# Three hand-written orders per engine in place of two, with the experts' bias product behind the small tiles, in a software-pipelined four-layer kernel

## The reference

```python
x = x + xattn0(layernorm(x), ctx, ctx)   # 16 heads of 8, biases
x = x + moe(layernorm(x))                # 8 experts, top 2, relu
x = x + xattn1(layernorm(x), ctx, ctx)   # 16 heads of 8, no biases
x = x + cell(layernorm(x))               # 64 steps over the rows of a group
# moe: scores = xf @ W_gate + b_gate; w = top-2 scores at their experts, else 0
#      h = relu(xf @ W1[e] + b1[e]); out = sum_e w[e] * (h @ W2[e] + b2[e])
# cell, one step, batch of 64:
#      f = sigmoid(xt @ wf.T + c @ uf.T + bf); i = sigmoid(xt @ wi.T + c @ ui.T + bi)
#      g = tanh(xt @ wc.T + c @ uc.T + bc);    c = f * c + i * g
# after the last step: h = tanh(x @ wo.T + c_final @ uo.T + bo)
```

## Time and profile before

| what | value |
|---|---|
| median of three runs | 847.08 us |
| the three runs | 846.52, 847.08, 849.42 us |
| span of the profiled execution, first to last instruction | 848.5 us |
| TensorE products, busy | 822.1 us (97%) |
| ScalarE busy | 783.1 us (92%) |
| VectorE busy | 769.7 us (91%) |
| GpSimd busy | 686.1 us (81%) |

### The profile page before, as it was taken

How to read it: one execution, slowest core, us unless ns; L and a number is a source line. 1 busy time by engine, 2 the same in 40 slices (tenths; PEclk the granted TensorE clock), 3 DMA queues, 4 the chain that set the end, 5 groups by cost and what they waited for, 6 DMA issues and landing times. The chain is left out here.

```text
span 848.5 us, 41475 instructions
## 1 busy us (share of the span) xinstructions
PE 822.1 (97%) x15268; PEld 739.4 (87%) x15268; DVE 769.7 (91%) x2778; ACT 783.1 (92%) x2490; POOL 686.1 (81%) x1292
## 2 busy tenths in 40 slices
PE   7899999999999999999999999999999999999996
PEld 4688898999999999999999899999998988888784
DVE  5689999999999999999999999999999998999755
ACT  4899999999999999999999999999999999988864
POOL 4788998888888888888888888888888887877634
PEclk7899999999999999999999999999999999999999
DMA  9400000000000000000000000000000000000005
GB/s 348 166 2 3 2 3 4 3 3 4 3 4 3 3 3 3 4 3 4 3 3 3 3 4 3 3 4 3 3 3 3 4 3 3 3 4 3 3 3 199
DMA packets 6965, 17.67 MB, mean 21 GB/s; under 512 B 752, under 2 KB 2288, under 8 KB 6768
## 3 DMA queue, kind: packets, MB, share of 16 engines
q1 hardware_dynamic: 6336, 14.36, 4.4%
q10 hardware_dynamic: 432, 0.68, 0.2%
HBM read 10.84 MB, written 4.19 MB: 18 GB/s over the span
## 5 line engine op out<-in xcount | busy, mean ns | idle before, releaser
L976 DVE TENSOR_REDUCE mx<-ps 128x8 f32<-128x512 f32 (+1 forms) x288 | 166.8, 621 | 11.9 <-PE ps L366 11.8
L1305 POOL TENSOR_TENSOR h<-Ex 128x512 f32<-128x512 f32 (+1 forms) x144 | 166.0, 1153 | 10.7 <-ACT Ex L734 8.1
L990 DVE TENSOR_TENSOR Ex<-ps,mx 128x512 f32<-128x512 f32 (+1 forms) x288 | 167.4, 622 | 0.0
L745 ACT ACTIVATE ET<-ps 128x512 f32<-128x512 f32 (+1 forms) x288 | 155.3, 573 | 11.1 <-PE ps L381 8.9
L734 ACT ACTIVATE Ex<-Ex 128x512 f32<-128x512 f32 (+1 forms) x288 | 163.8, 596 | 0.0
L1082 DVE SCALAR_TENSOR_TENSOR acc<-ps,we,acc 128x128 f32<-128x128 f32 x448 | 150.9, 337 | 11.9 <-PE ps L467 0.5
L783 ACT ACTIVATE hT<-ps,w 128x128 f32<-128x128 f32 x512 | 149.0, 400 | 4.7 <-PE ps L446 4.6
L381 PE MATMUL ps<-w,Ex 128*128 128x128 f32 x1024 | 149.8, 275 | 1.5 <-ACT qT L722 0.7
L446 PEld LDWEIGHTS ps<-xT,w 128*128 128x128 f32 x1024 | 124.1, 191 | 24.8 <-issue 24.6
L446 PE MATMUL ps<-xT,w 128*128 128x128 f32 x1024 | 142.2, 282 | 0.0
L467 PE MATMUL ps<-w,hT 128*128 128x128 f32 x1024 | 139.5, 281 | 0.3 <-DVE Ex L990 0.3
(11 more groups left out here) (108 smaller groups left out, 1793.7 us busy)
## 6 DMA issues: line engine op xcount, KB each, us to landing
cx<-ctx_dram SPq DMA_DIRECT2D x7, 512.0 KB, 12.3
x<-x_dram SPq DMA_DIRECT2D x7, 512.0 KB, 14.1
out_dram<-x SPq DMA_DIRECT2D x14, 256.0 KB, 2.7
w<-weights_dram SPq DMA_DIRECT2D x2, 512.0 KB, 5.8
w<-weights_dram SPq DMA_DIRECT2D x1, 576.0 KB, 8.5
out_dram<-x SPq DMA_DIRECT2D x4, 128.0 KB, 2.6
w<-weights_dram ACTq DMA_DIRECT2D x1, 328.0 KB, 5.2
w<-weights_dram ACTq DMA_DIRECT2D x1, 256.0 KB, 3.1
```

Source lines behind the costliest of these rows:

```text
L745: e.activation(ET[:, j % 2, r, lo:hi, :, :], b[:, 256 * lo:256 * hi].rearrange("p (c w q) -> p c w q", c=hi - lo, w=2), ACT.Copy).then_inc ...
L976: e.tensor_reduce(mx[:, j % 2, r, 4 * lo:4 * hi], b[:, 256 * lo:256 * hi].rearrange("p (j k) -> p j k", k=64), AX.X, ALU.max).then_inc(sig ...
L990: e.tensor_tensor(Ex[:, j % 2, r, 256 * lo:256 * hi].rearrange("p (j k) -> p j k", k=64), b[:, 256 * lo:256 * hi].rearrange("p (j k) -> p ...
L1305: e.tensor_tensor(u, v[:, :, :, 0:32], v[:, :, :, 32:64], ALU.add).then_inc(sig("half1"), 1)
```

## The change

Each engine gets three lists in place of two, for rounds 0 to 14, 15 to 71 and 72 to 79 (`STARTS`), with new orders in all of them, new lags where an operation moved from the end of a list to its head, and a new `AHEAD` with an entry for each of the three parts. `USES` has three tables. In TensorE's list of the full rounds `sA` comes before `pv`, `yb` comes right behind them and before `y0`, `q` and `rt` come between `gate` and `turnw`, and `e1` stands where `e0` stood. The pieces of b2 (`bias_pieces`) and the sum into `bo0` still stand at the head of VectorE's round, but the list behind them begins with `mx0` in place of `sb1`. No operation is added or taken out; no shape changes. `out_inputs` counts its groups from `OUT` = 73, the same round as before.

```diff
-FULL, LATE = FIRST, NT + -1
+STARTS = (0, 15, 72)
+FIRST, LAST = STARTS[0], 80
+OUT = NT + 9
 ...
 def phase(i):
-    return 0 if i < FULL else 1 if i < LATE else 2
+    return max(sum(i >= s for s in STARTS) - 1, 0)
 ...
+AHEAD = {"y0": (0, 0, -1), "wx0": (-1, -2, 1), "turnx": (0, 0, -1), "e1": (0, 0, -1), "p": (0, 0, -1),
 ...
```

More of the change, by code:

```diff
@@ L221, in build @@
         for i in range(FIRST, LAST):
-            for name, reader, lag, chain, step, first in (USES_LAST if i >= LATE else USES):
+            for name, reader, lag, chain, step, first in USES[phase(i)]:
                 made = 0
@@ L232, in build @@
                         made += 1
-                place += max(made, 1)
+                place += max(made, i >= 0)
         def bank_of(name, j):
@@ L499, in inputs_share @@
                 if m == 0:
-                    for name, reader, _, chain, step, first in USES:
+                    for name, reader, _, chain, step, first in USES[0]:
                         if name != "turnx":
@@ L589, in tensor_program @@
                     keys_values(r)
-            for i in range(LATE, LAST):
+            for i in range(STARTS[2], LAST):
+                for r in due(i, "turnw"):
+                    turn_w(r)
+                for r in due(i, "gate"):
+                    gate(r)
+                for r in due(i, "h0"):
+                    hidden(r, 0)
+                for r in due(i, "e1"):
+                    turn_e(r, 1)
+                for r in due(i, "p"):
+                    project(r)
+                for r in due(i, "turnx"):
+                    turn_x(r)
+                for r in due(i, "y1"):
+                    experts(r, 1)
@@ new lines, in tensor_program @@
+                for r in due(i, "h1"):
+                    hidden(r, 1)
+                for r in due(i, "e3"):
+                    turn_e(r, 3)
+                for r in due(i, "xin"):
+                    cell_inputs(r)
+                for r in due(i, "S"):
+                    scores(r)
+                for r in due(i, "sA"):
+                    step(r, 0)
+                for r in due(i, "pv"):
+                    values(r)
+                for r in due(i, "rt"):
+                    turn_r(r)
@@ L598, in tensor_program @@
+                for r in due(i, "wx0"):
+                    out_inputs(r, 0)
                 for r in due(i, "sB"):
                     step(r, 1)
[L600 to L610, removed]
@@ L626, in tensor_program @@
[L626 to L630, removed]
+                for r in due(i, "yb"):
+                    expert_bias(r)
             for n in (5, 6):
@@ L834, in scalar_program @@
                     e.wait_ge(sig("cell"), 1)
[L835 to L840, removed]
-                    exps(r, 0)
+                for r in due(i, "xo1"):
+                    out_inputs(r, 1)
+                for r in due(i, "re1"):
+                    relus(r, 1)
+                for r in due(i, "gB"):
+                    gates(r, 1)
+                for r in due(i, "sc"):
+                    scale(r)
                 for r in due(i, "ex1"):
                     exps(r, 1)
+                for r in due(i, "kvc"):
+                    keys_values(r)
+                for r in due(i, "ET3"):
+                    turn_e(r, 3)
                 for r in due(i, "qc"):
@@ L857, in scalar_program @@
                     turn_w(r)
+                for r in due(i, "ex2"):
+                    exps(r, 2)
+                for r in due(i, "xo0"):
+                    out_inputs(r, 0)
+                for r in due(i, "gA"):
+                    gates(r, 0)
+                for r in due(i, "rT"):
+                    turn_r(r)
+                for r in due(i, "ex3"):
+                    exps(r, 3)
+                for r in due(i, "re0"):
+                    relus(r, 0)
+            for i in range(STARTS[1], STARTS[2]):
+                for r in due(i, "re1"):
+                    relus(r, 1)
+                for r in due(i, "sc"):
+                    scale(r)
+                for r in due(i, "kvc"):
+                    keys_values(r)
+                for r in due(i, "ex0"):
+                    exps(r, 0)
+                for r in due(i, "gA"):
+                    gates(r, 0)
+                for r in due(i, "ET3"):
+                    turn_e(r, 3)
+                for r in due(i, "xT"):
+                    turn_x(r)
+                for r in due(i, "ET1"):
+                    turn_e(r, 1)
+                for r in due(i, "wd"):
+                    widen(r)
+                for r in due(i, "xo1"):
+                    out_inputs(r, 1)
+                for r in due(i, "ET0"):
+                    turn_e(r, 0)
+                for r in due(i, "ex1"):
+                    exps(r, 1)
+                for r in due(i, "ex2"):
+                    exps(r, 2)
+                for r in due(i, "ET2"):
+                    turn_e(r, 2)
+                for r in due(i, "qc"):
+                    query(r)
+                for r in due(i, "rT"):
+                    turn_r(r)
+                for r in due(i, "weT"):
+                    turn_w(r)
+                for r in due(i, "xo0"):
+                    out_inputs(r, 0)
+                for r in due(i, "gB"):
+                    gates(r, 1)
+                for r in due(i, "ex3"):
+                    exps(r, 3)
+                for r in due(i, "re0"):
+                    relus(r, 0)
@@ L1170, in vector_program @@
-                for r in due(i, "gidx"):
-                    gate_index(r)
+                for r in due(i, "sb0"):
+                    differences(r, 0)
+                for r in due(i, "c5"):
+                    combine(r, 5)
+                for r in due(i, "c7"):
+                    combine(r, 7)
+                for r in due(i, "mx1"):
+                    maxima(r, 1)
+                for r in due(i, "mx2"):
+                    maxima(r, 2)
+                for r in due(i, "st0"):
+                    stats_inputs(r)
```

443 lines of the change are left out of this document (264 added, 179 removed), and 73 rows, old and new, of tables (AHEAD, LAG, USES, USES_LAST).

## The result

| | median us | lowest to highest | runs |
|---|---|---|---|
| before, beside it | 847.20 | 846.52 to 849.42 | 5 |
| changed | 842.06 | 840.55 to 844.32 | 5 |

The ratio is 0.9933, interval 0.9914 to 0.9952: the change takes 5.1 us off where 4.3 were forecast. The profiled execution of the changed kernel has a span of 838.8 us and a time of 840.55, the shortest of the five. Before's profiled span of 848.5 thus belongs to a time of some 850.3, longer than all five of the table. The two profiles differ by 9.7 us, 4.6 of them because each lies at its own end of the scatter.

A forecast was written before the change was run, and what follows sets the result against it. TensorE's instructions in their order were taken to bound full rounds, a chain through all engines the start. Terms +4.8 - 3.9 - 0.8 - 3.5 - 0.9 = -4.3 us, from 847.08 to 843; range 836 to 852.

The forecast's parts named there:

- rival 3: Full rounds: q is late, so scores waits each round; at 0.3 us a round 857; chance 0.17.
- rival 1: Full rounds: array partly hides q's and h0's loads, round 11.98 to 12.0, 838; chance 0.24, shared with a better start.
- (a): Full round, yb moved ahead of y0: uncovered loads 0.16 after and 0.16 before, worth nothing, -0.01 to +0.06.
- (d): Full round: sA ahead of pv, e1 ahead of p and e0, the two wx calls: neighbours of one kind, 0.
- (b): Full round, gate: q's f32 load now follows its 8-column product and is uncovered, +0.075 (0.03 to 0.10).
- (c): Full round, turnw: h0's full products follow in place of two transposes, 0.33 against 0.29, +0.04.
- Rival 4: Full rounds: yb's bf16 load costs the 0.10 of an f32 one, 0.06 more a round, 846; chance 0.07.
- -0.8 for rounds 64 to 71: Eight rounds now in the full order: one run of small tiles fewer, -0.2, less 0.10 each; 0 to -1.6.
- the earlier wx0: Last rounds: wx0 issued one round earlier, its first eight products fill TensorE's idle time near 789; -0.9 (+2 to -2).
- rival 2: Start gives nothing, as several chains at once hold its rounds: 846.5, no measurable change; chance 0.16.
- (f): Start, rounds 4 to about 8: ex0 after xT (-0.3) and gate after e2 alone (0.15), 0.45 x 5 rounds = -2.2.
- (e): Start, VectorE: pieces of b2 and bo0 sum leave the softmax run for idle time before scores lands, -1.3.

The follow-up runs named there:

- second pair of profiles: Both kernels profiled again, unchanged: the changed kernel 841.52 us (ratio 0.9929), the kernel before 847.62 us (0.9999).
- the run with the wrong banks: Changed kernel with yb put back behind e3 in both program and bank table (USES[1]): 1044.56 us, ratio 1.2321.

## Why the prediction came out right, step by step

**The full round: right, 12.08 forecast and 12.085 measured.** (The +4.8 takes 0.10 a round for the 0.105 of the sum; 48 of these are 5.0.) All engines follow; no wait stands in the steady rounds (rival 3 is out, and so is rival 1). Of its terms: (a) yb, 0, measured -0.04, and (d) sA ahead of pv, 0, measured +0.03, by the run with yb back and the old banks: two errors of some 2 us each over 57 rounds that cancel, which is luck. yb's load behind the small tiles, put at 0.05, adds 0.01 to yb's slot; the 0.05 by which y0's load sticks out was right. (b) q behind the gate, +0.075, measured +0.08 in its slot. (c) turnw ahead of h0, +0.04, measured +0.05 - 0.01. The versions with q alone and with q and turnw moved give it back in part and in full, 2.6 to 3.1 and 4.3 to 4.8 us. Rival 4 falls with (a). A rule of the Trainium skill ("TensorE: Matmul & The Clock Gate", section "LDWEIGHTS (loading the stationary operand)") gives a load's time by its columns alone; by it yb's load, taken to delay its product in full, would cost as much as y0's, and the four slots together would have grown by about 0.06. They shrank by 0.01, and by 0.04 against the run with yb back, so this trace doesn't bear out the rule for what a load costs here. How long the load itself lasts is another matter: its record behind gate is 0.12 us long, and its product starts 0.02 after it.

What step (a) got wrong is its reading of the edit. I priced yb's move as a matter of weight loads and of neighbours in TensorE's queue. The two runs with yb back show that more hangs on it elsewhere: c0's new place on VectorE needs yb early (0.8 us a round if it isn't, 49 us in all), and the bank table turns with it (with both, 2.6 us a round, 4.3 where the clock falls). "Every instruction is kept; only its neighbours change" held for the time of this change, not for this part of it alone.

**Rounds 62 and 63: right, -3.9 forecast, -3.9 in the second pair of profiles.** The changeover at 66 shows the cause by itself.

**The rest of the last third: too good.** -0.8 for rounds 64 to 71 was +0.1 between tiles 63 and 70 (0.0 in the first pair). The full-list rounds with fewer stages cost more at first (tiles 63 to 66, 34.5 in the changed kernel, where the last list takes 33.9) and as much less later. I had priced entries and exits of small tiles, not the two lists; what a saved run of small tiles gives there, no run shows. -0.9 for the earlier wx0 was -0.6 between tiles 70 and 76, but not by wx0: its first group comes 6.6 us behind tile 70, where the idle time of the earlier trace rows lay 1.9 us behind it. The whole last list is new, and which of its moves gives the 0.6 is open; at its start it costs 1.6 us, and gives back more in the next rounds. TensorE's waits in the 104 us up to tile 76 fell from 3.2 us to 2.6.

**The start: -3.5 forecast, -4.1 measured, by the wrong terms.** The -4.1 is one pair's: tile 14 is at 116.6 to 121.2 in four executions with the old first lists and at 114.6 and 115.3 in the changed kernel's two, so the gain is 1.3 us at the least and rival 2 is out by a little only. (f), -2.2, is worth nothing, as the run without it shows; by the rows, of a cycle through four engines I shortened a stretch that another branch of the same cycle, through GpSimd, ran beside. (e), -1.3, is under-sized: the move of the pieces is worth 2.0 us on the kernel before (0.4 to 2.8 by the interval), 1.4 to 2.6 on the changed one. By the profiles this goes with the clock. In all nine executions with the pieces ahead of mx0, on either kernel, the clock stood at half for 10.24 us of the start (in one of them in two stretches); in the five with the pieces in the softmax 20.48, 17.07, 20.48, 20.48 and 6.83. The last of these reached tile 4 as early as the nine. That the pieces' own 0.8 us is nothing and the clock all of it is thus likely, and not shown: no run set the clock apart. The remaining 1.6 to 1.8 come between tiles 9 and 14, where every version with the new first lists takes 52.4 to 52.6 and every one with the old list 54.1 to 54.2. TensorE's waits there are 2.3 us for Ex, Km and wep in the old list and 1.0 in the new one. km0's place alone is not the cause; which of the other moves is stays open.

**The pauses: left at 0, and the change is not their cure.** The 29 gaps sum to 3.5 us in the profile before and to 2.3, 1.1, 1.3 and 1.6 in the four other executions of its full list; with the new list to 0 in three executions and to 0.9, 1.1, 1.2 and 2.0 in four. The means are 2.0 and 0.7, so of the change's 5 us one may come from here, by chance or by the new order: so few executions don't tell. I took them for something of sA; they come where TensorE waits for its next block of 256 instructions.

In sum, +4.8 - 3.9 - 0.8 - 3.5 - 0.9 = -4.3 became +2.2 (5.1 for 47 longer rounds, less 2.3 of pauses and 0.6 of small differences) - 3.9 + 0.1 - 4.1 - 0.6 = -6.3 by the second pair, and -5.1 to -6.1 by the medians. The forecast time was good partly by luck: the gain that (f) didn't bring came from (e) and from tiles 9 to 14, for which nothing was forecast, the last rounds gave less and the pauses more, and inside the round (a) and (d) cancel.

## What to carry to other kernels

Where TensorE is full and never waits, price an order by its neighbours: here a full product behind one of 8 columns, or behind a lone short one, cost 0.05 to 0.08 us more, so put another short product there; that alone was worth 4.3 to 4.8 us. In a chain that goes round through several engines, a shorter leg gives nothing until every leg that runs beside it is shorter too, so look what the next instruction of the freed engine waits for. An operation's early place on one engine may serve its consumer's place on another, and in a bank table by turns moving one group gives others another bank: move such pairs together, or not at all.

## What was unexpected in the hardware

TensorE's small tiles (24 products in 0.34 us, two instructions each) can outrun the fetching of instructions: pauses of 0.3 to 0.7 us, always at one place of a block of 256 instructions, in some rounds and not in others, and not in all the same ones when the same kernel runs again. Each ends 1.21 to 1.58 us after the packet with the next block has landed. The Trainium skill ("Runtime: NRT & Kernel Launch", section "Instruction fetch mechanics") describes blocks of 256 instructions and calls their fetch hidden behind the rate of issue; the block size agrees with these places, the hiding doesn't hold here. It was not tried whether fewer instructions, or a larger spacing of the small tiles, takes the pauses away.

The half clock at the start lasts 6.8 to 20.5 us in executions of one and the same first list; in the run with the wrong banks, where TensorE waits 2.3 us of each round, the clock falls again and again, as the profile's row of the clock in tenths shows:

```profile
PEclk8999999999999999999999989999999899899999
```
